# Placing the first twelve score units of each attention among the pieces of the row maxima

## What is computed

```python
x = x + _L0_attn_a_ref(_layernorm(x, axis=-1), ...)   # 16 heads of 8, plus a shared rotary part of 32
x = x + _L0_ffn_ref(_layernorm(x, axis=-1), ...)      # 8 experts of 512, 257 tokens each
x = x + _L0_attn_b_ref(_layernorm(x, axis=-1), ...)   # 16 heads of 8, causal
x = x + _L0_ffn_ref(_layernorm(x, axis=-1), ...)
```

## Time and profile before

| | us |
|---|---|
| median of 3 runs | 1162.95 (1161.97 to 1165.49) |
| profiled execution | 1163.28 |
| span of its trace | 1161.6 |
| PE busy | 1001.9 (86%) |
| VectorE busy | 736.8 (63%) |
| ScalarE busy | 682.8 (59%) |
| GpSimd busy | 228.1 (20%) |

### The profile page before, as it was taken

How to read it: one execution, slowest core, us unless ns; L and a number is a source line. 1 busy time by engine, 2 the same in 40 slices (tenths; PEclk the granted TensorE clock), 3 DMA queues, 4 the chain that set the end, 5 groups by cost and what they waited for, 6 DMA issues and landing times. The chain is left out here.

```text
span 1161.6 us, 15698 instructions
## 1 busy us (share of the span) xinstructions
PE 1001.9 (86%) x5536; PEld 666.4 (57%) x5536; DVE 736.8 (63%) x1325; ACT 682.8 (59%) x1159; POOL 228.1 (20%) x488
## 2 busy tenths in 40 slices
PE   1848999999997899889956699999999769997997
PEld 0325555555544666678834355555555356675885
DVE  6637677776744555559873567776766165654996
ACT  0313566666665678568822156666666647775884
POOL 4013445553332000000006022222222200000000
PEclk9956999999999799989978599999999959998999
DMA  3394432342102011354306321222100021125541
GB/s 82 79 249 96 112 90 81 105 110 83 56 38 91 1 37 37 80 156 132 70 1 163 73 29 28 29 29 29 29 1 2 9 83 37 37 40 146 147 106 37
DMA packets 67246, 82.44 MB, mean 71 GB/s; under 512 B 6200, under 2 KB 55264, under 8 KB 66400
## 3 DMA queue, kind: packets, MB, share of 16 engines
q1 hardware_dynamic: 64944, 80.24, 28.1%
q10 hardware_dynamic: 2224, 1.20, 0.5%
HBM read 58.48 MB, written 22.68 MB: 70 GB/s over the span
## 5 line engine op out<-in xcount | busy, mean ns | idle before, releaser
L1162 PE MATMUL f_banks<-f_xr,f_w1r 128*128 128x512 f32 x768 | 207.5, 419 | 15.0 <-DMA f_w2r<-scratch_w 15.0
L1248 ACT ACTIVATE f_h<-f_banks,b_t 128x512 f32<-128x512 f32 x228 | 149.7, 682 | 79.0 <-PE f_banks L1162 58.2
L1162 PEld LDWEIGHTS f_banks<-f_xr,f_w1r 128*128 128x128 f32 x768 | 147.0, 196 | 57.2 <-issue 26.0
L1178 PE MATMUL f_banks<-f_hr,f_w2r 128*128 128x512 f32 x684 | 169.9, 394 | 9.0 <-DVE f_hr L1302 9.0
L905 DVE TENSOR_REDUCE b_mlate<-b_banks 128x2 f32<-128x1024 f32 (+3 forms) x120 | 124.8, 1079 | 60.1 <-PE b_banks L773 44.3
L905 DVE TENSOR_REDUCE a_mlate<-a_banks 128x2 f32<-128x1024 f32 (+3 forms) x120 | 124.7, 1079 | 59.4 <-PE a_banks L773 43.4
L1302 DVE TENSOR_TENSOR f_hr<-f_h,f_hr 128x1024 fp32r<-128x1024 f32 (+1 forms) x128 | 141.2, 1105 | 26.1 <-ACT f_hr L1255 24.3
L1178 PEld LDWEIGHTS f_banks<-f_hr,f_w2r 128*128 128x128 f32 x684 | 126.4, 188 | 35.7 <-DVE f_hr L1302 7.6
L765 PE MATMUL a_banks<-a_k,a_q 120*128 120x512 f32 (+3 forms) x384 | 107.9, 386 | 25.0 <-POOL a_k L718 12.0
L1255 ACT ACTIVATE f_hr<-f_h 128x1024 fp32r<-128x1024 f32 (+1 forms) x128 | 123.9, 968 | 4.1
L808 PE MATMUL b_banks<-b_q,b_k 121*128 121x512 f32 (+3 forms) x384 | 116.4, 386 | 9.9 <-DMA b_q<-b_mt 8.7
(11 more groups left out here) (215 smaller groups left out, 1198.7 us busy)
## 6 DMA issues: line engine op xcount, KB each, us to landing
scratch_w<-a_tab SPq DMA_DIRECT2D x16, 512.0 KB, 3.1
f_w1r<-scratch_w SPq DMA_DIRECT2D x16, 512.0 KB, 6.1
f_w2r<-scratch_w SPq DMA_DIRECT2D x16, 512.0 KB, 6.3
v<-scratch_gate SPq DMA_DIRECT2D x32, 256.0 KB, 5.1
xt<-scratch_gate SPq DMA_DIRECT2D x32, 256.0 KB, 5.3
a_rot<-in_w SPq DMA_DIRECT2D x16, 256.0 KB, 4.3
scratch_q<-a_q_hl SPq DMA_DIRECT2D x24, 128.0 KB, 3.1
scratch_k<-a_k_hl SPq DMA_DIRECT2D x24, 128.0 KB, 3.1
```

What stands on the lines that cost most here:

```text
L1162: last = pe.matmul(h_ps[:, j, :], w1r[e % 2][:, wp, j * P:(j + 1) * P], xr[xp][:, chunk(c)], start=(i == 0), stop=(i == 2))
L1178: last = pe.matmul(y_ps[:, q % 2, :], w2r[e % 2][:, wp, j * P:(j + 1) * P], hr[q % 2][hp][:, j, :], start=(j == 0 and i == 0), stop=(j == ...
L1248: act.activation(to, h_ps[:, j, :], ACT.Gelu, bias=m.b1_t[:, e * HB + j:e * HB + j + 1]).then_inc(gelu_done, 1)
```

## The change

The target that ends the filling of a unit's list is now another one in half 0. Instead of `done + LEAD` it rises in twelve equal steps from 11264 columns, over 12190 behind unit 0, to what it is from half 1 on. So fewer pieces stand behind unit 0 and more behind units 1 to 11. Nothing is added or taken away, and from unit 12 on the lists are the same.

```diff
-LEAD = 17000
+LEAD, START = 17000, 11264
...
+    half = sum(set_tiles(HALVES[0][1], v // GH)[1] for v in range(NU[0]))
     for i, (n, c) in enumerate(HALVES):
         for v in range(NU[i]):
             done += set_tiles(c, v // GH)[1]
             beside[UNIT0[i] + v] = []
-            while at < len(order) and cols < done + LEAD:
+            most = START + (v + 1) * (half + LEAD - START) // NU[0] if i == 0 else done + LEAD
+            while at < len(order) and cols < most:
```

## The result

| | before | after |
|---|---|---|
| median of 22 runs each, us | 1162.60 (1159.12 to 1168.06) | 1167.65 (1161.23 to 1171.35) |
| ratio to before, 95% interval | | 1.0037, 1.0025 to 1.0050 |
| profiled execution, us | 1163.28 | 1164.23 |
| span of its trace, us | 1161.6 | 1162.5 |

The ratio stands for 2.9 to 5.8 us, 4.3 in the middle. Single executions of either kernel spread over some 10 us, so one trace proves little: the two profiled ones are only 0.95 us apart. What follows therefore compares short stretches of several traces.

The account below looks back on a forecast made before the run. PE, busy 86% of the span, was taken to bound the kernel. Shifts of -0.4 us plus +4.6 us for the low clock gave +4.2 on the median 1162.95: 1167.1 us, 8-in-10 range 1161.5 to 1171.0.

Parts of the forecast that it names:

- The standstill: Ahead of unit 12 in each attention: PE stands still 2.3 to 3.5 us because covering work went ahead of the turn.
- The price of the clock: Behind the wait for unit 12: low clock costs 1.7 to 2.95 us per attention, 2.3 taken, +4.6 for both.
- the 4 to 6 us of low clock that I gave as a sign: Behind the wait ahead of unit 12: granted clock 0.50 in the 1-us windows for 4 to 6 us.
- The shift in a: Start of unit 12 in attention a against 111.46: -0.9 us at the high clock, +0.6 at the low.
- The walk itself: Attention a, steps from GpSimd's masks to unit 12: start at 110.6 at the high clock, 112.1 at the low.
- The 110.8 that I gave for the row of maxima in a: Attention a before the change: row of maxima there at 110.8, 4.67 us behind the turn at 106.13.
- The shift in b: Start of unit 12 in attention b: -0.6 us at the high clock, +1.3 if it falls again by (2, 0).
- The sum of the shifts: Unit 12's start, both attentions together: -1.5 to +1.9 us without the case of no rise, -0.4 taken.
- the clock survives the wait: Rival 1, at the wait ahead of unit 12: no clock price, only the shifts, 1161.5 to 1164.9 us; chance 0.20.
- The point I gave: Deciding point for rival 1: longest standstill left ahead of unit 12 no longer than the 1.04 us at 102.13.
- rival 2: Low spell outlasts 6.3 us, or in b the clock never rises before the turn: 1171 to 1174 us; chance 0.12.

Follow-up runs that it names:

- second trace of after: The changed kernel, nothing altered, run once more for another trace: 1171.65 us in one run.
- late turn alone: Kernel before, turn of half 1 moved behind unit 10 and pieces (2, 2), (2, 3) behind unit 11: 1167.27 against 1163.01 us, ratio 1.0032.
- trial with twelve: Kernel before plus twelve matmuls nobody reads ahead of unit 0 in each attention: 1161.52 against 1163.01 us, ratio 0.9997.

## Why the prediction was right, and where it wasn't

I predicted 1167.1 us and slower; 1167.65 was measured. The sum was +4.2 us and the ratio gives +4.3. The mechanism was the one forecast: a standstill ahead of unit 12 with a low clock behind it. That the sum agrees to 0.1 us is luck, since the parts agree less well.

- **The standstill** was right. Forecast 2.3 to 3.5 us ahead of unit 12, ended by a DMA; measured 3.30 in a (0.97 and 2.33) and 3.18 in b (0.97 and 2.21). From the end of the copy to unit 12 it is 3.58 us in b (668.81 to 672.39), as in the earlier trace rows, and 3.68 in a. In the second trace of after it was smaller in a, 0.68 and 1.18 us, since the work behind the turn ran at the low clock and took longer.
- **The price of the clock** was right in kind and too high. The term that was mis-sized is the length of the low spell: I took 3.8 to 6.3 us from the three rises of before and so 2.3 us for each attention. The spells in the trace of after last 3.4 us and cost about 1.6 each, not the 4 to 6 us of low clock that I gave as a sign; one of 6.8 us, in its second trace, cost 2.64. Over six beginnings with the new order, unit 12 to the third group of values takes 7.88, 8.20, 7.92 in a and 7.89, 8.97, 7.93 in b, on average 8.13 against the 6.33 of the traces where the clock holds: 1.8 each, 3.6 for both where 4.6 stood. One of the six, the 8.20, is the spell that began at GpSimd's wait.
- **The shift in a** was wrong in sign, by a misread row. I took the row at 111.46 in the earlier trace rows for unit 12. It holds units 13 and 14. Unit 12 is the last of three units merged into one row of that timeline:

```profile
110.23 0.88 PE L808 MATMUL a_banks<-a_q,a_k 121*128 121x256 f32 x3
```

 and started at about 110.6. The walk itself ended near the truth: it gave 110.6 at the high clock and 112.1 at the low one, and 111.87 came, with the values at the low clock (1.94 us; I had 2.0). Measured against 110.6 it would have read 0 to +1.5 us, where I wrote -0.9 to +0.6. Over three traces each, unit 12 comes 1.5 us later behind unit 0, and 1.3 by its moment in the span. The 110.8 that I gave for the row of maxima in a falls with the same row: it was there by 110.6.
- **The shift in b** was better than both walks. Forecast -0.6 to +1.3, measured -1.5 in the first trace and -1.1 over three. The clock rose at 658.9 (0.56 in the window of 658), at the early end of the 659 to 661.4 that I gave, and held up to (2, 0). What I had missed is that (1, 12) then ends earlier too: VectorE's seven reductions took 7.02 us without a stop, where I had left its end as before.
- **The sum of the shifts**, -0.4 by choice, is +0.4 over the traces. Two mistakes of opposite sign nearly cancelled. With the measured terms it is +0.4 + 3.6 = +4.0, or +3.8 with attention a's shift by its moment; the interval, 2.9 to 5.8, holds both.
- **The rivals.** That the clock survives the wait happened, in one beginning: attention b of the kernel with the late turn alone, after 2.14 us. In the same trace the same order lost the clock in a, after 2.27 us, so it belonged into the price as a weight. Whether it can happen with the changed kernel's order isn't shown: in all five beginnings where that order had its stop of 2.2 to 2.3 us, with 0.97 us ahead of it, the clock fell. The point I gave, stops up to 1.04 us, was too strict: the clock also held after 1.05, 1.16 and 1.58 us in other kernels. A low clock that lasts on (rival 2) shows in the second trace of after, with 8.97 us, but is not what the median shows.
- **The Trainium skill**, page "TensorE: Matmul & The Clock Gate", section "Why this matters for your kernels", names long gaps as what brings the clock down and closing them as the remedy. The runs bear the remedy out: ten matmuls in each gap moved the ratio from 1.0037 to 0.9998. That only long gaps count, they don't: with the short stops among the pieces the clock was 0.50 up to 668.2 us in b, 19.3 us behind unit 0, without them it rose at 658.9, 9.6 us behind. In b of the ten traces without filling ahead of unit 0 it rose 8.5 to 12.7 us behind unit 0 with the spread pieces, and with the old places 19.3 to 19.4 us behind three times, but 12.6 once (the late turn alone). So with the short stops the clock mostly stays low for longer, not always.
- **One number ahead of the prediction** is off: the new target behind unit 0 is 12168 columns, not 12190. The table of the order is right.

## What to carry to other kernels

A turn of data through another engine and a DMA needs work behind it on the engine that will wait; work that an order moves ahead of the turn is no longer cover, even if nothing else is later. On PE such a standstill can cost twice, once as the wait and once by the clock behind it, and a handful of matmuls nobody reads can be cheaper than the gap. If they end long before the wait does, 5.07 us in the trial with twelve, the clock is low again when the work begins. Before a row is taken for a given instruction, count: timelines merge neighbours, and the instruction looked for may be the last of three in the row above. Where single executions differ by more than the change is worth, compare the same short stretch in several traces.

## What the runs showed of the hardware

- The fall of the clock is not tied to the moment of the stop. In the first trace of after it came 0.15 us (b) and 0.9 us (a) after PE had begun again, in the kernel with the new order in a alone 1.5 us after (0.66 in the window of 114, unit 12 at 112.81), in that with it in b alone 1.6 us after (678.2, unit 12 at 676.64), in the second trace of after, in b, within the stop itself (679.7). Where it comes after the stop, the first unit looks undisturbed and the work behind it pays.
- Low spells behind nearly the same stop last differently: 3.4 us five times, 6.8 us once. One that began behind a wait for GpSimd lasted 13.7 us (102.8 to 116.5, second trace of after).
- Nearly equal stops end differently: 2.21 to 2.33 us brought the clock down in six beginnings, 2.14 us in one did not, nor did 1.05, 1.16 and 1.58.
- At the low clock eight products with the values take 1.94 us, at the high one 1.06.
- The transfers of the first turned maxima in attention b kept PE waiting for 5.33 us in one execution of the changed kernel and 11.71 in another; over the ten traces without filling there it was 5.09 to 11.71.
- The same stream of pieces with the same short stops ended its low clock 19.3 us behind unit 0 in one kernel and 12.6 us in another (before, and before with the late turn; attention b).
